# Attention layer of a graph network: one softmax maximum per tile within a batch, and three of four carried sums moved to ScalarE

## The reference, cut to what matters

```python
alpha = einsum('ehk,k->eh', leaky_relu(scores), pk)   # score of an edge, per head
seg = et * N + dst                                    # edge type and target node
m = segment_max(alpha, seg)
a = exp(alpha - m[seg])
denom = segment_sum(a, seg)
msg = (xj * (a / denom[seg])[..., None])              # 32 channels of each of 4 heads
out = segment_sum(msg * edge_importance[et], dst)
```

## Time and profile before

| | us |
|---|---|
| timed runs (3), median | 8602.15 (8601.02 to 8606.16) |
| the profiled execution: span from first to last instruction | 9989.8 |
| stretch that holds layer 0's attention | 440 to 2020 of the span |
| TensorE matmul busy over the span | 4658.3 (47%) |
| VectorE busy over the span | 5136.0 (51%) |
| ScalarE busy over the span | 1546.3 (15%) |
| GpSimd busy over the span | 5819.3 (58%) |

### The profile page before, as it was taken

One profiled execution on the slowest core, in us unless ns is written; L12 is line 12 of the kernel. 1 busy time (PEld: TensorE's weight loads), 2 busy tenths in 40 slices (PEclk: granted clock), 3 DMA queues, 4 the chain that ended last, 5 costly groups with the idle time before them and its releaser, 6 DMA issues. The chain is left out here.

```text
span 9989.8 us, 82305 instructions
## 1 busy us (share of the span) xinstructions
PE 4658.3 (47%) x14536; PEld 2840.5 (28%) x14536; DVE 5136.0 (51%) x11795; ACT 1546.3 (15%) x3063; POOL 5819.3 (58%) x5427
## 2 busy tenths in 40 slices
PE   6287777733233322222322225566666566444443
PEld 5133333222222212221222122333333333333332
DVE  6387787755555444544454454444444433333333
ACT  1211111121111211111211112111111112000002
POOL 2466666536666466656466562555555534888885
PEclk8688888855555655555555555778778786555555
DMA  2432323443333233333333332444444441444445
GB/s 68 126 61 55 56 57 56 50 112 85 83 82 86 71 84 83 93 86 83 77 89 87 86 89 62 123 123 127 125 122 128 123 80 24 36 36 36 36 36 100
DMA packets 658400, 804.99 MB, mean 81 GB/s; under 512 B 289379, under 2 KB 496662, under 8 KB 657175
## 3 DMA queue, kind: packets, MB, share of 16 engines
q0 software_dynamic: 317424, 531.92, 26.9%
q1 hardware_dynamic: 340902, 272.29, 9.0%
HBM read 575.15 MB, written 228.61 MB: 80 GB/s over the span
## 5 line engine op out<-in xcount | busy, mean ns | idle before, releaser
L1767 POOL DMA_INDIRECT big<-table_layer,slot_records_L x2400 | 2325.7, 969 | 1615.9 <-DMA slot_records_L<-slot_records 861.3
L1786 PE MATMUL own_ps_L<-of_tile_L,big 50*128 50x16 f32 x1224 | 284.0, 370 | 2804.4 <-DVE fade_L L1871 2522.3
L2408 POOL DMA_INDIRECT sums_by_source<-msg,to x800 | 1252.4, 1565 | 260.7 <-issue 189.4
L981 POOL DMA_INDIRECT big<-table_layer,idx_L x912 | 951.1, 1043 | 619.5 <-issue 285.8
L2045 PE MATMUL ps<-big,w 128*128 128x512 f32 x1792 | 957.9, 685 | 341.6 <-ACT big L2064 208.4
L1786 PEld LDWEIGHTS own_ps_L<-of_tile_L,big 50*128 50x128 f32 x1224 | 272.0, 324 | 2879.5 <-issue 2865.1
L2014 POOL DMA_INDIRECT big<-table_layer,rec_m x904 | 877.5, 971 | 275.4 <-issue 272.0
L2101 DVE SCALAR_TENSOR_TENSOR big<-ps,nbb,big 128x128 f32 x1792 | 545.8, 346 | 914.0 <-remote 658.9
L1057 PE MATMUL sums_L<-h,ident 128*128 128x512 f32 x1344 | 716.4, 683 | 188.9 <-DVE h L1137 166.6
L1893 DVE TENSOR_TENSOR_SCAN big<-h,products_L 128x1122 f32<-128x1122 f32 x300 | 747.6, 2492 | 24.6
L2350 PE MATMUL psM<-h,same 128*128 x1600 | 413.8, 440 | 643.2 <-issue 640.1
(11 more groups left out here) (440 smaller groups left out, 7501.0 us busy)
## 6 DMA issues: line engine op xcount, KB each, us to landing
hidden_edge_parts<-big SPq DMA_DIRECT2D x72, 768.0 KB
hidden_edge_parts<-big SPq DMA_DIRECT2D x72, 640.0 KB
big<-table_layer,slot_records_L POOLq DMA_INDIRECT x2400
h<-in_edges SPq DMA_DIRECT2D x75, 384.0 KB
h<-in_edges SPq DMA_DIRECT2D x72, 320.0 KB
table_layer<-xr SPq DMA_DIRECT2D x49, 298.0 KB
big<-table_layer,idx_L POOLq DMA_INDIRECT x912
big<-table_layer,rec_m POOLq DMA_INDIRECT x904
```

What stands on the lines that cost most here:

```text
L981: G.indirect_dma_start(out=g[b][:, u, s, :], out_offset=None, in_=table, in_offset=bass.IndirectOffsetOnAxis(ap=at, axis=0)).then_inc(gath ...
L1767: G.indirect_dma_start(out=ring[b][:, s, :], out_offset=None, in_=tab1_d[l], in_offset=bass.IndirectOffsetOnAxis(ap=fl[q][:, at + s, R_POS ...
L1786: last = PE.matmul(own_ps[:, c * SLOTS:(c + 1) * SLOTS], own1T[:, c * P:(c + 1) * P], of_tile[b % 2][:, :], start=True, stop=True)
L2408: G.indirect_dma_start(out=sum_d[s], out_offset=bass.IndirectOffsetOnAxis(ap=to[u][:, s:s + 1], axis=0), in_=msg[u][:, s, :], in_offset=No ...
```

## The change

In words:

1. `maxima` gets a second scan, over the same data reversed, which carries the last maximum of a tile back to the tile's earlier items of the batch. The result `last_max` is the same for all items of one tile within one batch. For the scan `lift` gets one more element behind it (`lifts`), and `last_max` lies in free room of `h`.
2. With it the factor of a carried sum within the batch no longer depends on the column: it is exp(lift), which is 1 where the tile goes on and 0 where it ends. Only the first item of a batch still has a factor per lane and column. The exponents are laid out accordingly: a sum of 16 elements, a copy of 48, a subtraction of 64 and one of 16, in place of three operations on 64.
3. `carry_on` stays on VectorE for u = 0 alone. For u = 1, 2, 3 ScalarE makes `carry` by `pass_on`: a copy of the PSUM bank, 512 columns, with one factor per lane. A new semaphore, `passed_on`, tells TensorE.
4. ScalarE's order becomes: `js`, keep 0, pass_on 1, keep 1, pass_on 2, keep 2, `exps(k + 1)`, pass_on 3, keep 3, `shrinks(k + 1)` (the exponential L1000, split from `exps`), `lay_slots(k + 1)`.

```diff
+                    def shrinks(k, b):
                         act.wait_ge(shr_arg, k + 1)
                         A.activation(shrink[b][:, :, :, :], shrink_arg[:, :, :, :], ACT.Exp).then_inc(shr_ok, 1)
...
+                    def pass_on(k, b, u):
+
+                        act.wait_ge(summed, k * B + u + 4)
+                        A.activation(carry[u % 2][:, :], sums[b][u - 1][:, 0:T * D], ACT.Copy,
+                                     scale=shrink[b][:, 0, 0, u + 1:u + 2]).then_inc(passed_on, 1)
+
                     with act.Fori(0, n) as i:
                         for b in range(2):
                             k = i * 2 + b
-                            exps(k + 1, 1 - b, i + b)
...
                             act.wait_ge(z_ok, k + 1)
                             for u in range(B):
-                                act.wait_ge(carried, k * B + u + 1)
+                                if u:
+                                    pass_on(k, b, u)
+                                else:
+                                    act.wait_ge(carried, k + 1)
                                 act.wait_ge(kept, k * B + u + 2 * B)
                                 keep(js[u], run_z[b][:, :, u], sums[b][u - 1] if u else sums[1 - b][B - 1])
+                                if u == 2:
+                                    exps(k + 1, 1 - b, i + b)
+                            shrinks(k + 1, 1 - b)
                             lay_slots(1 - b, i + b)
...
-                                pe.wait_ge(carried, (i * 2 + b) * B + u + 1)
+                                if u:
+                                    pe.wait_ge(passed_on, (i * 2 + b) * (B - 1) + u)
+                                else:
+                                    pe.wait_ge(carried, i * 2 + b + 1)
                                 PE.matmul(sums[b][u][:, 0:T * D], ident[:, :], carry[u % 2][:, :],
                                           start=False, stop=True, skip_group_check=True).then_inc(summed, 1)
...
                         dve.drain()
+                        V.tensor_tensor_scan(flat(last_max)[:, ::-1], lifts[:, 1:][:, ::-1],
+                                             flat(run_max[:, :, :])[:, ::-1], 0.0, ALU.add, ALU.max)
                         dve.wait_ge(shr_ok, k + 1)
-                        V.tensor_tensor(shrink_arg[:, 1, :, 1:B + 1], item_max[:, :, 1:B + 1], run_max[:, :, 1:B + 1],
+                        V.tensor_tensor(shrink_arg[:, 0, :, 1], run_max[:, :, 0], lift[:, :, 1], ALU.add)
+                        V.tensor_copy(shrink_arg[:, 0, :, 2:B + 1], lift[:, :, 2:B + 1])
+                        dve.drain()
+                        V.tensor_tensor(shrink_arg[:, 1, :, 1:B + 1], item_max[:, :, 1:B + 1], last_max[:, :, 1:B + 1],
                                         ALU.subtract)
-                        V.tensor_tensor(shrink_arg[:, 0, :, 1:B + 1], run_max[:, :, 0:B], lift[:, :, 1:B + 1], ALU.add)
-                        dve.drain()
-                        V.tensor_tensor(shrink_arg[:, 0, :, 1:B + 1], shrink_arg[:, 0, :, 1:B + 1],
-                                        run_max[:, :, 1:B + 1], ALU.subtract).then_inc(shr_arg, 1)
+                        V.tensor_tensor(shrink_arg[:, 0, :, 1], shrink_arg[:, 0, :, 1], last_max[:, :, 1],
+                                        ALU.subtract).then_inc(shr_arg, 1)
...
                             weigh(k, b, 0)
-                            carry_on(k, b, 0)
+                            carry_on(k, b)
                             weigh(k, b, 1)
                             weigh(k, b, 2)
-                            carry_on(k, b, 1)
                             if ahead:
                                 scores(i + b, 1 - b)
-                            carry_on(k, b, 2)
                             weigh(k, b, 3)
                             if ahead:
                                 maxima(k + 1, 1 - b)
-                            carry_on(k, b, 3)
```

More of the change, by code:

```diff
@@ L858, in gnn, with attention @@
         h = sb("h", [P, NTP, D])
-        def attention(tag, T, table, own, acc, g, prod, zt):
+        def attention(tag, T, table, own, acc, g, prod, zt, last_max):
             L = T * H
@@ L882, in attention @@
                 sc = [sb(f"sc_{tag}{b}", [P, B, S, L], fp32, ph) for b in range(2)]
-                lift = sb(f"lift_{tag}", [P, L, B + 1], fp32, ph)
+                lifts = sb(f"lift_{tag}", [P, L * (B + 1) + 1], fp32, ph)
+                lift = lifts[:, 0:L * (B + 1)].rearrange("p (l u) -> p l u", u=B + 1)
                 item_max = sb(f"item_max_{tag}", [P, L, B + 1], fp32, ph)
@@ L914, in attention @@
                 summed = sem(f"products_summed_{tag}")
-                carried = sem(f"sum_before_shrunk_{tag}")
+                carried = sem(f"batch_before_shrunk_{tag}")
+                passed_on = sem(f"item_before_passed_on_{tag}")
                 z_ok = sem(f"exponential_sums_ready_{tag}")
@@ L1027, in _ @@
                     exps(0, 0, 0)
+                    shrinks(0, 0)
                     lay_slots(0, 0)
+                    def pass_on(k, b, u):
+                        act.wait_ge(summed, k * B + u + 4)
+                        A.activation(carry[u % 2][:, :], sums[b][u - 1][:, 0:T * D], ACT.Copy,
+                                     scale=shrink[b][:, 0, 0, u + 1:u + 2]).then_inc(passed_on, 1)
                     with act.Fori(0, n) as i:
@@ L1145, in weigh, with carry_on @@
                         last.then_inc(prods, 1)
[L1147 to L1153, removed]
+                    def carry_on(k, b):
+                        dve.wait_ge(summed, k * B + 4)
+                        V.tensor_tensor(carry[0][:, :].rearrange("p (l c) -> p l c", c=C),
+                                        sums[1 - b][B - 1][:, 0:T * D].rearrange("p (l c) -> p l c", c=C),
+                                        bc(shrink[b][:, 0, :, 1], 2, C), ALU.mult).then_inc(carried, 1)
                     def weights(k, b):
@@ L1176, in _ @@
                     V.memset(run_max[:, :, :], LOW)
-                    V.memset(lift[:, :, :], -BIG)
+                    V.memset(lifts[:, :], -BIG)
                     V.memset(shrink_arg[:, :, :, :], LOW)
@@ L1242, in scratch @@
                     "p (u s w) -> p u s w", u=B, s=S) if T > 1 else None
-                return prod, zt
+                last = 2 * n + B * S * T4 * H * K5
+                last_max = hf[:, last:last + T * H * (B + 1)].rearrange("p (l u) -> p l u", u=B + 1)
+                return prod, zt, last_max
             def moments(dve, a, z):
```

## The result

The changed kernel takes 8595.85 us (median of 18 runs, 8587.44 to 8605.20) against 8608.03 (18 runs) of the kernel before: ratio 0.9985, interval [0.9979, 0.9992]. A second comparison gave 8591.9 against 8600.35, ratio 0.9989 [0.9980, 0.9999]. So 12 and 8 us are gained by the medians. Forecast were 8597 us.

What follows compares the result with a forecast made beforehand. VectorE bounds the batch from carry to W, then waits for TensorE's fourth item, whose clock takes VectorE's gain back. +0.05 x 56 = +3, less 8 for lateness, is -5 us: 8602 - 5 = 8597 us, range 8530 to 8625.

Steps and rivals of the forecast that it cites:

- VectorE's gain: Three carries leave VectorE, gaining 1.20 us, and `maxima` grows by 0.30: 0.90 us a batch, 50 us in 56.
- The third carry was free: VectorE's carry for u = 3, before `weights`: removing it gains 0, since `weights` waits for ScalarE's exponential anyway.
- From the carry to the fourth item's end: VectorE's stretch from the first carry to the end of the fourth item's products: 17.44 - 1.20 = 16.24 us.
- stray lateness: Small lateness of VectorE and loads, absorbed by the longer wait before the carry: 0.14 us a batch, 8 us in 56.
- The pause and the clock: TensorE pauses once, about 3.5 us; its clock falls and delays the fourth item, so VectorE waits 1.63 us, not 0.69.
- W: The moment in a batch when VectorE ends the fourth item's products; the next first carry was forecast at 7.63 us after.
- the time to full clock: TensorE's time from resuming after its pause to full clock, 2.4 GHz: taken as 5.9 us, as before the change.
- the slack: ScalarE's spare time before `shrinks` is wanted, after its new copies and keeps: 1.8 us.
- the stalls: VectorE's 26 long waits at the carry before `scores`, 140.2 us in all: taken as the profiler's and left out.
- Rival two: The stalls at the carry are real in timed runs and most of 140 us comes back: about 8480 us, chance 0.06.
- +3 is the batch: A whole batch takes 23.87 us against 23.82: +0.05 x 56 = +3 us.

Runs made afterwards that it cites:

- the work behind the carry: Changed kernel plus two unused VectorE multiplications, about 1.1 us a batch, in the second item's products: ratios 0.9920 and 0.9902 to the kernel before, on slower chips.
- the control: The changed kernel itself, run again without further edits on the chip of 8600: 8591.9 us against 8600.35 of the kernel before, ratio 0.9989.
- the filled kernel: Changed kernel plus four unused matmuls in TensorE's pause: 8521.49 us against 8609.71 of the kernel before, ratio 0.9892; on slower chips 1.0012, 1.0025, 1.0018.
- the kernel before with the same filling: Kernel before plus four unused matmuls behind the third item's products on TensorE: 10015.85 us against 10000.51, ratio 1.0018, on a slower chip.

## Why the prediction was right, step by step

- **VectorE's gain.** From L1139 to the release of `shrink_arg` the changed `maxima` takes 597.31 to 598.59, 1.28 us; 1.36 was worked out, and 1.05 before. `weights` follows the fourth item's end (597.39) after 1.71 us instead of 1.48: +0.23, forecast +0.30. The small operations take 0.17 to 0.23 and overlap more than I allowed. The third carry was free, as said: its place is now the wait of 0.5 us for ScalarE.
- **From the carry to the fourth item's end.** 580.92 to 597.39 is 16.47 us, 16.43 in the median of the stage; forecast 16.24. The term was mis-sized by the batch that I chose: its 17.44 lay 0.18 below what the 24.0 us of the five batches give. Those 0.18 us I had counted as stray lateness, of which the longer gap would absorb 0.14 a batch, the 8 us of the sum. No run shows such an absorption.
- **The pause and the clock.** Forecast: one pause of about 3.5 us, full clock 5.9 us after resuming, the carry at W + 7.63, a gap of 1.63. Measured: 3.76 us, 5.5 us (573.61 to 579.10), and from W to the carry 1.71 + 5.77 = 7.48 us in the median of the stage, a mean gap of 1.55 (80.5 over 52). The batch is 23.9, forecast 23.87.
- **Where the number owes something to luck.** The carry came 0.15 us sooner behind W than forecast and W came 0.19 later behind the carry, and the two cancel. The sum also takes the time to full clock as fixed at 5.9 us. The runs show 5.5 and 4.0, and a pause of 3.60 us without a fall. With the work behind the carry, a fixed time would give 25.0 us a batch; measured were 24.05.
- **That the clock is the cause**, and not a wait that only goes with it, is shown twice on the chip of 8600: by the run with extra matmuls, where TensorE gets more work, only its pause and its clock change for the better, and the wait disappears; and by the control's second batch, where the pause stays, the clock doesn't fall, and the wait is gone too.
- **ScalarE.** Its new copy is 0.68 us. The page "ScalarE: Activation LUTs" of the Trainium skill, in its section on ACT_TABLE_LOAD, gives 93 ns for a factor read per lane; the trace agrees, 681 against 585 ns of the plain copy in the same trace. ScalarE then waits 1.94 us for `shrink_arg` before its exponential (598.63), the slack that was forecast as 1.8. Its order delays nobody at the level of 8600.
- **What was wrong: the stalls.** I took them, and the 1388 us between the profile and the timed runs, for the profiler's. They belong to the chip: on three of the four chips the timed runs take 10,000 us too and every profile has the stalls, while on the chip of 8600 the profiled execution of the changed kernel has a span of 8597.7 us beside a median of 8595.85. So the profile of before came from a slower chip than its timed runs, and the stalls don't account for the whole difference: they are some 3.4 us a batch in this stage, 190 of 1388 us. Rival two, that they are real in timed runs, was thus true on those chips and of no effect in the result. Its price of -120 us was not seen either where the carries were on ScalarE and the pause was filled: the stalls only moved.
- **The size.** Forecast -5 us, measured -12 and -8. Of the -5, +3 is the batch and -8 the absorbed lateness, which no run shows, so the sign was forecast by its weakest term. If the stage alone accounts for the gain, the kernel before would take some 24.1 us a batch on the chip of 8600; it has no profile there, so this is worked out only.

## What to carry to other kernels

Work taken off the busiest engine helps only if the engine that it meets next keeps pace. Here TensorE's clock fell in its pause. A lighter VectorE and an earlier carry merged its two pauses, 3.24 and 0.46 us, into one of 3.76, and the eight product passes of the fourth item took 6.42 us instead of 5.35, where 3.60 are possible. Before you move work, ask what TensorE will do in the time that you free. If it has nothing, a few matmuls without use may be worth more than the edit: 8 to 12 us came from the change alone and 70 to 84 more from the filling on top of it. Together they are the best version seen, 1.08% faster than the kernel before. What the filling alone would give in the kernel before on that chip was not measured. Check on which chip a gain was measured: on three of four chips this best version gained nothing.

## What the runs showed of the hardware that had not been expected

- **Chips differ by 16%.** The same kernel takes 8600 to 8610 us on one chip and 10,000 on three. At the slower level there are stalls of 5 to 15.5 us, at one place of the loop or another, and in the filled kernel they take back what the shorter batches give: 22.3 us undisturbed, 27.2 in the mean. Their cause is open, but the traces have one clue. In this stage ScalarE's sequencer (which runs its register, branch and semaphore instructions) has 76 to 342 instructions that take 0.66 to 0.74 us each in the traces from the slower chips, and SyncE's has 188 to 440; in the three from the chip of 8600 there is none. The same instruction of the same kernel, shortest, median and longest in ns, first on a slower chip, then on the chip of 8600:

```profile
L1022 ACTq FUSED_REGOPS  x225: 13/37/699, 487.8 to 1979.7; - x113
L1022 ACTq FUSED_REGOPS  x225: 37/42/43, 435.6 to 1693.4; - x113
```

- **Slower work, faster kernel.** On those chips, 1.1 us of useless VectorE work behind the carry made the kernel 0.8 to 1.0% faster, twice, and its mean batch 25.2 and 25.3 us instead of 27.3. The same work before the carry made it 0.5 to 0.6% slower. The two faster runs are also those with the fewest long ScalarE sequencer instructions (92 and 76; the others on such chips have 156 to 342). What causes what is not shown.
- **Batches of one length where the clock falls in each.** They take 24.0, 23.9 and 24.05 us in three kernels whose VectorE gaps are 0.7, 1.5 and 0.5 us. The clock's record has falls 23.89 us apart in all three (587.29 and 611.18, 572.29 and 596.18, 897.89 and 921.78). The full level came back 5.9, 5.5 and 4.0 us after TensorE resumed. Where the clock stays up, the length follows VectorE's work: 22.3 us in the filled kernel, 23.4 in the kernel before with the same filling, 23.4 with the extra work before the carry. Why the falls keep this distance while VectorE's work differs is not shown.
- **A pause does not always drop the clock.** In one trace and one kernel, a pause of 3.60 us left it at 2.4 GHz and one of 3.57 us did not.
